# One-hots of the first counting stage in bfloat16, the edge weight as a sum of three bfloat16 parts

## What is computed

```python
x = x + gat(relu(layernorm(x)), edge_index)                                   # 4 heads
x = x + filtered_sum(relu(layernorm(x)), edge_attr_20, edge_index)
x = x + gated(relu(layernorm(x)), src, dst, edge_weight, edge_weight_n2)
x = x + gat_twice(relu(layernorm(x)), edge_index)
```

## Time and profile before

| | us |
|---|---|
| Median of 3 runs | 6361.24 (6352.69 to 6371.05) |
| The profiled execution's own time | 6352.34 |
| Its span in the trace | 6349.1 |
| Counting stage, first to last matmul of L1553 | 1,513 to 2,166 |
| Busy over the span: PE, DVE, POOL, ACT | 4763.1, 4615.4, 2965.5, 2165.1 |

### The profile page before, as it was taken

The page is one execution under the profiler, slowest core; times in us unless marked ns, Lnnn a source line. Parts: engine busy times, 40 slices in busy tenths (PEclk is TensorE's granted clock), DMA queues, the critical chain, the costliest instruction groups (busy, mean ns, idle before and its releaser), DMA issues.

```text
span 6349.1 us, 81975 instructions
## 1 busy us (share of the span) xinstructions
PE 4763.1 (75%) x22785; PEld 3319.6 (52%) x22785; DVE 4615.4 (73%) x5602; ACT 2165.1 (34%) x3980; POOL 2965.5 (47%) x3112
## 2 busy tenths in 40 slices
PE   7826999994999633577774777777778999964548
PEld 4415888873888533233333656666666555451213
DVE  9796776444999699899996888888875000159796
ACT  5633343332555143455552222222205000133223
POOL 0077777777777777882002777777730000000000
PEclk9999999997999855799996887888788999957777
DMA  9993444445999799653224666666641444136573
GB/s 244 278 239 81 140 139 139 138 137 189 311 310 312 256 341 327 215 163 91 71 73 139 217 215 218 216 217 221 216 91 51 150 153 150 39 84 218 176 228 126
DMA packets 695980, 1161.89 MB, mean 183 GB/s; under 512 B 268058, under 2 KB 483589, under 8 KB 681702
## 3 DMA queue, kind: packets, MB, share of 16 engines
q1 hardware_dynamic: 327403, 534.89, 29.2%
q0 software_dynamic: 134656, 328.87, 16.7%
q10 hardware_dynamic: 233594, 293.96, 13.4%
HBM read 672.47 MB, written 484.93 MB: 182 GB/s over the span
## 4 chain that ended last, share of the span: by engine, by line
PE 31%; DVE 30%; POOL 18%; issue 11%; DMA 6%; SPq 1%; ACT 1%; ACTq 1%; DVEq 0%; POOLq 0%
POOL slots_by_block_pair L962 13%; PE psall L1553 10%; PE psall L1704 8%; DVE arena L2287 6%; DVE arena L2297 6%; DVE arena L2258 6%; DMA arena<-table_x,arena 5%; POOL arena L995 4%; PE psall L1637 4%; DVE arena L2351 3%; DVE arena L2514 3%; POOL idle L964 1%; PE psall L1411 1%; PE psall L1668 1%; PE psall L1476 1%
## 5 line engine op out<-in xcount | busy, mean ns | idle before, releaser
L995 POOL DMA_INDIRECT arena<-table_x,arena x856 | 956.2, 1117 | 825.7 <-DMA arena<-slots_by_src 548.3
L962 POOL DMA_INDIRECT slots_by_block_pair<-arena x806 | 827.8, 1027 | 573.6 <-DVE arena L2039 314.6
L1614 PE MATMUL psall<-arena 128*65 128x313 f32 (+1 forms) x2800 | 867.9, 453 | 263.7 <-DVE arena L2297 263.7
L984 POOL DMA_INDIRECT slots_by_src<-arena,pos_s x806 | 918.5, 1140 | 253.8 <-issue 231.9
L1637 PE MATMUL psall<-arena 128*125 128x256 f32 x1712 | 571.6, 506 | 354.4 <-DVE arena L2351 354.4
L1154 ACT ACTIVATE arena<-psall 128x500 f32<-128x500 f32 (+3 forms) x668 | 306.1, 465 | 1372.9 <-PE psall L1649 1047.9
L1614 PEld LDWEIGHTS psall<-arena 128*65 128x65 f32 (+1 forms) x2800 | 337.4, 130 | 793.2 <-DVE arena L2297 404.8
L1520 PE MATMUL psall<-shared_w,arena 128*128 128x256 f32 x3264 | 750.4, 383 | 1.4 <-DVE arena L2191 1.4
L1553 PE MATMUL psall<-arena 128*128 128x250 f32 x2880 | 626.2, 377 | 105.8 <-DVE arena L2238 79.5
L1637 PEld LDWEIGHTS psall<-arena 128*125 128x125 f32 x1712 | 434.3, 260 | 468.6 <-DVE arena L2351 374.4
L1520 PEld LDWEIGHTS psall<-shared_w,arena 128*128 128x128 f32 x3264 | 605.7, 191 | 75.9 <-DVE arena L2191 1.6
(11 more groups left out here) (331 smaller groups left out, 7037.0 us busy)
## 6 DMA issues: line engine op xcount, KB each, us to landing
arena<-slots_by_src SPq DMA_DIRECT2D x107, 1040.0 KB
filters<-arena ACTq DMA_DIRECT2D x204, 520.0 KB, 2.7
arena<-filters POOLq DMA_DIRECT2D x202, 520.0 KB, 5.9
slots_by_src<-shared_on SPq DMA_DIRECT2D x8, 9230.0 KB, 77.5
weights_out<-arena ACTq DMA_DIRECT2D x125, 320.0 KB, 3.1
arena<-counts SPq DMA_DIRECT2D x50, 781.5 KB, 4.3
counts<-arena ACTq DMA_DIRECT2D x125, 312.5 KB
weights_in<-arena ACTq DMA_DIRECT2D x125, 312.5 KB
```

The source lines that it names most:

```text
L962: G.indirect_dma_start(slots_c, bass.IndirectOffsetOnAxis(ap=pos_c[:, j, q:q + 1], axis=0), rec_c[:, c, :], None).then_inc(s["scattered_c" ...
L984: G.indirect_dma_start(slots_s, bass.IndirectOffsetOnAxis(ap=pos_s[:, c:c + 1], axis=0), ring_s[:, g % SLOTS, c % TG, :], None).then_inc(r ...
L995: G.indirect_dma_start(hg[:, f % 2, j, :], None, t_x1, bass.IndirectOffsetOnAxis(ap=pay_s[:, f % 2, j, S_IDX:S_IDX + 1].bitcast(I32), axis ...
L1614: last = MM(ps[gat_bank(n, wn, h_, c)][0:F + 1, 0:z - a], rows, g["e1"][:, q % g["RE"], a:z], start=(b == 0), stop=(b == NT - 1))
```

## The change

All in the counting stage. The place numbers are kept as bfloat16, each twice side by side (`twice`), and the row 0 to 127 as well (`row_2`, copied to PSUM as `row_p`). The weight is split into three bfloat16 numbers whose sum is exact (`w_parts`: high, mid, low), each kept twice, and copied to PSUM. This is done by seven DVE instructions (`run_records`) for each 14 steps (`RUN_S`), in place of the three copies ahead of the first step. DVE still issues three instructions a step, with bfloat16 in and out; the third makes all three weighted one-hots at once. The two one-hot instructions compare numbers by twos, and a row of destinations has 126 columns, of which 125 are used. TensorE issues three bfloat16 matmuls for each tile: counts and high part (250 columns), then the mid and the low part (125 columns each), the last two at the address of the half plus 125. Only the third adds to `cb_mm`.

```diff
-                        MM(psall[:, bass.ds(half_at(mine[k], j), 2 * P)], ohs[sl][:, TG * k + j, :],
-                           ohw[sl][:, TG * k + j, :, :].rearrange("p a k -> p (a k)"),
+                        at, by_s = half_at(mine[k], j), ohs[sl][:, TG * k + j, :]
+                        MM(psall[:, bass.ds(at, 2 * P)].rearrange("p (a k) -> p a k", a=2), by_s,
+                           count_and_weight(sl, TG * k + j),
+                           start=False, stop=False, skip_group_check=True)
+                        MM(psall[:, P:][:, bass.ds(at, P)], by_s, ohw[sl][:, TG * k + j, 1, 0:P],
+                           start=False, stop=False, skip_group_check=True)
+                        MM(psall[:, P:][:, bass.ds(at, P)], by_s, ohw[sl][:, TG * k + j, 2, 0:P],
                            start=False, stop=False, skip_group_check=True).then_inc(s["cb_mm"], 1)
...
-            for n in range(0, W_STEPS, IN_RUN):
-                width = CT_G * min(IN_RUN, W_STEPS - n)
-                last = V.tensor_copy(psall[:, weights_at(n):weights_at(n) + width],
-                                     pay_c[:, CT_G * n:CT_G * n + width, C_W])
-            link(last)
+            link(V.tensor_copy(row_2.bitcast(BF16), iota[:, :]))
+            link(V.tensor_copy(row_p, row_2))
+
+            def run_records(run):
+
+                t0, n = RUN_T * run, min(RUN_T, T1 - RUN_T * run)
+                of = pay_c[:, t0:t0 + n, :]
+                for c, at in ((0, C_S), (1, C_D)):
+                    V.tensor_copy(twice[:, run % 3, c, 0:n, :], of[:, :, at:at + 1].to_broadcast([LANES, n, 2]))
+                high, mid, low = (w_parts[:, c, 0:n, :] for c in range(3))
+                rest = w_rest[:, 0:n]
+                link(V.tensor_copy(high, of[:, :, C_W:C_W + 1].to_broadcast([LANES, n, 2])))
+                link(V.tensor_tensor(rest, of[:, :, C_W], high[:, :, 0], ALU.subtract))
+                link(V.tensor_copy(mid, rest.unsqueeze(2).to_broadcast([LANES, n, 2])))
+                link(V.tensor_tensor(low, rest.unsqueeze(2).to_broadcast([LANES, n, 2]), mid, ALU.subtract))
+                link(V.tensor_copy(run_weights(run), w_twice))
...
-                V.tensor_tensor(ohd, by_d, of_tiles(pay_c, C_D, at, P), ALU.is_equal)\
+                V.tensor_tensor(by_twos(ohd[sl]), row(EVEN), paired(1, EVEN), ALU.is_equal)\
                     .then_inc(s["cb_oh"], 1)
-                V.tensor_tensor(ohs[sl], by_s, of_tiles(pay_c, C_S, at, LANES), ALU.is_equal)\
+                V.tensor_tensor(by_twos(ohs[sl]), row(LANES), paired(0, LANES), ALU.is_equal)\
                     .then_inc(s["cb_oh"], 1)
                 turn_wait(dve, s["cb_oh"], 3, CT_R, it, sl, c=1)
-                weights = psall[:, weights_at(n):weights_at(n) + CT_G]
-                V.tensor_tensor(wdd, ohd, weights.unsqueeze(2).to_broadcast([LANES, CT_G, P]),
+                weights = run_weights(run).bitcast(BF16).rearrange("p (t u) -> p t u", u=2)[:, 3 * t0:3 * (t0 + CT_G)]
+                V.tensor_tensor(ohw[sl].rearrange("p j a (k u) -> p (j a) k u", u=2),
+                                ohd[sl].unsqueeze(2).to_broadcast([LANES, CT_G, 3, EVEN]),
+                                weights.unsqueeze(2).to_broadcast([LANES, 3 * CT_G, EVEN // 2, 2]),
                                 ALU.mult).then_inc(s["cb_oh"], 1)
```

More of the change, by code:

```diff
@@ L94 @@
 LASTS = NB // 4
+RUN_S = 512 // (3 * CT_G)
+RUN_T = RUN_S * CT_G
 assert 4 * LASTS + 1 == NB and T1 < 2048
@@ L253, in gnn_kernel @@
         o_tab = o_wt + 5 * D + 4 * G3
-        assert o_stage + CT_G * LANES <= o_tab
         tables = view(o_tab, 1, TAB).bitcast(I32)
@@ L269, in gnn_kernel, with count_and_weight @@
         tjunk = view(o_e + 4 * EP, LANES, NB)
-        o_ohw = o_diag + HALF
-        o_both = o_ohw + 4 * CT_G * P
+        o_parts_1 = o_diag + HALF
+        o_both = o_parts_1 + 4 * CT_G * EVEN
         stage_both = view(o_both, LANES, 2 * 3 * PAIRS * P).rearrange("p (a b k) -> p a b k", a=2, k=P)
         assert o_both + 2 * 3 * PAIRS * P <= o_rec
[L275 to L280, removed]
+        o_parts_3 = o_b + 2 * NT * EVEN
+        assert T1 * C_REC <= 2 * NT * EVEN and 2 * CT_G * EVEN <= NT * EVEN
+        ohs = [view(o_oh_b + n * CT_G * LANES // 2, LANES, CT_G * LANES // 2).bitcast(BF16)
+               .rearrange("p (j k) -> p j k", j=CT_G) for n in range(CT_R)]
+        o_ohd = (o_parts_1, o_parts_1 + 2 * CT_G * EVEN, o_parts_3)
+        ohd = [view(o_, LANES, CT_G * EVEN // 2).bitcast(BF16).rearrange("p (j k) -> p j k", j=CT_G) for o_ in o_ohd]
+        ohw = [view(o_ + CT_G * EVEN // 2, LANES, 3 * CT_G * EVEN // 2).bitcast(BF16)
+               .rearrange("p (j a k) -> p j a k", j=CT_G, a=3) for o_ in o_ohd]
+        def count_and_weight(sl, j):
+            first_, apart_ = 2 * o_ohd[sl] + EVEN * j, CT_G * EVEN + 2 * EVEN * j
+            return arena[0:LANES, :].bitcast(BF16)[:, first_:first_ + 2 * apart_]\
+                .rearrange("p (a k) -> p a k", a=2)[:, :, 0:P]
+        o_twice = o_oh_b + CT_R * CT_G * LANES // 2
+        twice = view(o_twice, LANES, 3 * 2 * RUN_T).bitcast(BF16).rearrange("p (r c t u) -> p r c t u", r=3, c=2, u=2)
+        w_twice = view(o_twice + 6 * RUN_T, LANES, 3 * RUN_T)
+        w_parts = w_twice.bitcast(BF16).rearrange("p (t c u) -> p c t u", c=3, u=2)
+        w_rest = view(o_twice + 9 * RUN_T, LANES, RUN_T)
+        row_2 = view(o_twice + 10 * RUN_T, LANES, LANES // 2)
+        assert o_twice + 10 * RUN_T + LANES // 2 <= o_tab
         ctd = view(o_cb, LANES, 2 * N).rearrange("p (r s d) -> p r s d", r=2, s=NT)
@@ L487, in gnn_kernel, with run_weights @@
         run_w = ps[7][:, LANES:512]
-        IN_RUN = 512 // CT_G
-        def weights_at(n):
-            return 512 * (4 + n // IN_RUN) + CT_G * (n % IN_RUN)
+        row_p = ps[7][:, 0:LANES // 2]
+        row_b = row_p.bitcast(BF16)
+        def run_weights(run):
+            return ps[4 + run % 3][:, 0:3 * RUN_T]
         s = {n: sem(n) for n in """zeroed r_dve r_pe cleared consts in_edges in_ew in_x filled blank_c blank_s w_small w_more w_next  ln_stats link   go pool_go
@@ L2227, in pair_onehots, with paired @@
             def pair_onehots(n):
                 it, sl = divmod(n, CT_R)
-                ohd, wdd = ohw[sl][:, :, 0, :], ohw[sl][:, :, 1, :]
+                run, t0 = n // RUN_S, CT_G * (n % RUN_S)
+                if n % RUN_S == 0:
+                    run_records(run)
                 turn_wait(dve, s["cb_mm"], CT_G, CT_R, it, sl, back=CT_R, base_=1)
-                at = CT_G * n
-                V.tensor_tensor(ohd, by_d, of_tiles(pay_c, C_D, at, P), ALU.is_equal)\
+                def paired(c, width):
+                    return twice[:, run % 3, c, t0:t0 + CT_G, :].unsqueeze(2).to_broadcast([LANES, CT_G, width // 2, 2])
@@ L2233, in pair_onehots, with by_twos, row @@
+                def by_twos(ap):
+                    return ap.rearrange("p j (k u) -> p j k u", u=2)
+                def row(width):
+                    return row_b[:, 0:width].rearrange("p (k u) -> p k u", u=2).unsqueeze(1)\
+                        .to_broadcast([LANES, CT_G, width // 2, 2])
+                V.tensor_tensor(by_twos(ohd[sl]), row(EVEN), paired(1, EVEN), ALU.is_equal)\
                     .then_inc(s["cb_oh"], 1)
-                V.tensor_tensor(ohs[sl], by_s, of_tiles(pay_c, C_S, at, LANES), ALU.is_equal)\
+                V.tensor_tensor(by_twos(ohs[sl]), row(LANES), paired(0, LANES), ALU.is_equal)\
```

## The result

The changed kernel takes 6499.42 us in the median of 4 runs (6484.3 to 6502.37), the kernel before 6360.58: a ratio of 1.021, with an interval of 1.019 to 1.023, so 139 us more. The forecast was 6488 us and slower. PE in the profiles is TensorE, the engine of the matmuls, DVE is VectorE, ACT ScalarE, POOL GpSimd and SP SyncE. The traces record TensorE's granted clock at two levels, 1.00 and 0.50 (the high and the low clock of the prediction); PEclk is its mean over a stretch.

What follows compares the result with a forecast made beforehand. TensorE's sequencer was to bound the changed counting stage: tiles 645, L1549's successor 70, word loads 60 and ACT waits 5 make 780 us against 653. The added 127 us give 6361 + 127 = 6488 us, range 6440 to 6565.

Steps and rivals of the forecast that it cites:

- The bound of before: Counting stage before: TensorE's array bounds it, 621 us for 1,440 tiles, hiding most of the sequencer's 576 us.
- The array after: Changed tile's 500 bfloat16 columns: 0.22 us, 320 us in all; 0.40 a tile at the low clock, not the bound.
- The sequencer after: TensorE's register instructions, four a tile, plus three matmuls: 0.45 us a tile, 645 us; whole stage 780 us.
- The loads: Loads of the table's words on TensorE: 39 of 1.54 us with the following step, 60 us, now counted in full.
- Near 1.5 us: Sign expected in the changed kernel's profile: how long each load of the table's words takes.
- The prediction's bound of short loads: Lower bound for the table's word loads: 39 loads of 0.9 us would save 25 us.
- the fast rate: DVE's three bfloat16 instructions at 0.55 ns an element: 4.4 us, 4.65 a step with the records, hidden behind the sequencer.
- rival B: Counting stage: DVE at 1.04 ns an element throughout, stage 1,003 us, 350 more, time 6711; chance 0.08.
- What lies behind: Masks and attention wait for the last sums; POOL is not waited for there; the 127 us move through to the end.
- A: Counting stage: sequencer not the bound, DVE is; stage 558 us, 95 less, time 6266; needs tiles under 0.30 us; chance 0.07.
- C: Counting stage: only DVE's long instruction at 1.04 ns an element, stage 820 us, 167 more, time 6528; chance 0.06.
- D: Counting stage: word loads of 0.9 us, hidden matmul hand-over, 0.39 a tile; 16 us more, 6377, within 0.3%; chance 0.05.

Runs made afterwards that it cites:

- float32 run with two addresses: Kernel before, all float32, its matmul of 250 columns cut into two of 125, each with its own address: stage 794 us, time 6493.1 us (one run).
- the version with single elements: Changed kernel, DVE's three instructions reading each slot number and weight as one element repeated, not as a pair: stage 994 us, time 6687.6 us.
- one address: Changed kernel with a half's sums turned round so all three matmuls share an address: stage 631 us, 6315.5 us against 6340.0 before, ratio 0.995.
- the three faster versions: Edits of the changed kernel: one shared address (6315.5 us), mid and low matmuls left out (6310.3), shared address with one shift less per four tiles (6294.3).
- a third address: Changed kernel with an address instruction of its own for each tile's third matmul: stage 973 us, time 6659.0 us (one run).
- the last version: One-address version with table fields one bit lower, saving a shift for each four tiles: stage 596 us, 6294.3 us against 6349.1 before, ratio 0.992.
- the high part alone: Changed kernel without the matmuls of the mid and low parts: stage 612 us, time 6310.3 us (one run).

## Why the prediction was right

**The bound of before** was read rightly: PE busy 626 of the 653 us at a granted clock of 0.99, the array at 0.431 us a tile, with the sequencer hidden at 0.31. The float32 run with two addresses shows how thin that cover was: 0.13 us more on the sequencer, and the same columns take 794 us. It was thinner than the prediction's 576 us of sequencer work against 621: from its first to its last register instruction of the stage the sequencer took 649 us, 48 of them waits for a half to be emptied, so it had 601 of its own. Most of the 25 us between are small stops, below.

**The array after** was rightly left out. Each matmul beyond the first cost 0.007 us or less. In the changed kernel the granted clock was 0.86 in the mean, both levels in turn, and the tiles keep their pace at either. At the lower level, 0.50, busy time and clock, and the first matmuls of two tiles:

```profile
1830.00:1832.30 2.30, 2.22 (x15) 1.43 (x14) 2.30 (x3) 1.30 (x3) 1.69 (x3) 0.50 1.01 239
...
1831.44 0.39 PE L1573 MATMUL psall<-arena 128*128 128x250 bf16 x1
...
1831.88 0.39 PE L1573 MATMUL psall<-arena 128*128 128x250 bf16 x1
```

They start 0.44 us apart. From 1837.5 to 1841.0 us, where the granted clock is 1.00, it is 0.43 to 0.44 too, small stops aside (the last fence of this document). A duration is longer at the lower level, 0.39 us for 0.28, the pace is not.

**The sequencer after** was the sum's main term, 645 us for the tiles. The stage took 786; less L1568's 70, 53 for the loads and 5 of waits for ACT, the tiles took 658, 0.457 each where I had 0.448. The hand-over I took at 0.02 for each matmul is nearer to nothing beyond the first, and the instructions themselves were a little dearer: of the two address instructions the first is recorded with 42 ns and the second with 46, where L1553's had 37, and the steps behind them are 120 and 124 ns, where I had 0.097 us and the hand-over. What remains over is small stops, below.

**The loads** I had at 1.54 us with the step behind them, 60 in all; the median duration fell to 1.13 us, and the 39 cost 53 (1.35 each, since the mean lies above the median). "Near 1.5 us" was among the signs that I had named, and it did not come. The single line in the changed kernel:

```profile
L1560 PEldq TENSOR_LOAD <-arena x40: 845/1128/2803, 1453.1 to 2276.6; - x40
```

The prediction's bound of short loads, 0.9 us each, was 25 us off the sum, and the loads went a third of the way to it. They and the dearer tiles nearly cancelled (7 us less, 13 more), which is luck in so close a sum.

**DVE** took 0.947, 0.948 and 2.508 us, 0.95, 0.97 and 2.5 in the prediction, and its 4.4 us a step lay hidden. The choice of the fast rate was a choice: no row of before showed it, and 0.14 of the chances stood against it. With the row in PSUM, the 1,512 elements took 947 ns as pairs and 1,723 as single elements; from there to the third instruction's 4,536 (2,508 and 4,867 ns), whose weights lie in PSUM too, it is 0.52 and 1.04 ns an element. At 1.04 throughout the kernel would have been at rival B, as the version with single elements was.

**What lies behind** moved as a block: masks 372 us and attention 616, in both of which DVE is as full as before (busy 360 and 614 us, before 357 and 614). POOL, busy 253 us beside the attention, was busy 32: it had finished earlier in relation to the others, and that brought nothing. The other way round it did count: a faster counting stage pushes POOL's sorting into the attention, and in the profiled execution with one address the end of it was waited for. "Is not waited for there" held for the slower stage; of the three faster versions it failed in one profiled execution.

**The rivals.** A needed a tile under 0.30 us; even one register instruction less did not give that. B and C needed DVE without its pairs. D needed short loads and a tile of 0.39.

## What to carry to other kernels

Count what an engine's sequencer executes for each piece of work, at some 0.1 us for each register instruction here, and compare the sum with the engine's own time before making that shorter: this change halved the array's work (by the prediction's estimate, 0.22 us a tile for 0.431) and lengthened the stage by a fifth, for want of one shared address. Matmuls in a loop whose target is a register should share that register; laying out the sums so that all begin at one place was a change of ten lines and worth 155 us of the stage. And read a sequencer's pace from the starts of its instructions, since the durations (36 ns for a step of 97) hide nearly two thirds of it.

## What the runs showed of the hardware that was not expected

**The loads of words are longer in a faster stage.** The same 12 words took, at the median, 1.05 us with single elements (stage 994 us, DMA share 0.76), 1.06 with a third address (973, 0.77), 1.13 in the changed kernel (786, 0.83), 1.26 in the float32 version (794, 0.82), 1.48 before (652, 0.89), 1.65 in the last version (596, 0.91) and with the high part alone (612, 0.91), and 1.85 with one address (631, 0.90). The loads are longer where the DMA engines are fuller, and so the one-address version gave back some 20 us of its gain (39 x 0.52, by the means of 1.87 and 1.35 us with the step behind them). This is a relation over eight runs and no experiment. Within a run it shows as well: in the last 89 us of the changed kernel's stage (from 2,210 us, DMA share 0.54) the four loads took 0.85 to 0.99 us, the 35 ahead of them (share 0.87) 1.20 at the median; with one address the last three (share 0.53) took 0.85 to 1.07, the 36 ahead (0.94) 1.90. The pace of the tiles is the same there, so it is not the pace alone; but ACT had ended its work too, no run took only the traffic away, and what in it holds the load up stays open. The loads of the one-address version, from 0.85 to 3.0 us:

```profile
L1561 PEldq TENSOR_LOAD <-arena x40: 849/1853/3006, 1431.0 to 2132.2; - x40
```

**Small stops in the register instructions.** In the chain of the changed kernel the first matmuls of successive tiles stand 0.43 to 0.44 us apart, and at some places 0.47 or more, with no wait recorded (start us, us, what):

```profile
1837.51 0.28 PE psall L1573
1837.94 0.28 PE psall L1573
1838.38 0.28 PE psall L1573
1838.85 0.28 PE psall L1573
...
1840.51 0.28 PE psall L1573
1840.95 0.28 PE psall L1573
```

The undisturbed 0.437 us would make 629 us of the tiles; the stops are most of the other 29. The change did not make them: steps that are 20 ns or more over their median come every 1.25 us at the median in the changed kernel and every 1.26 in the kernel before, where they add up to some 22 us and were as good as hidden. No run here tells their cause.
